# Moving the low part of the output weights from VectorE to GpSimd, behind the last tiles that GpSimd normalises

## The reference, cut to what matters

```python
q = (x @ w_q)              # 32 heads of 128, with rotary embedding
k = (x @ w_k); v = (x @ w_v)   # 8 heads, each serves 4 query heads
lk = ((x @ w_lq) @ w_lk); lv = (x @ w_lv)   # a second, latent set of 32 heads
attn = causal_attn(q, k, v); lat = causal_attn(q, lk, lv)   # softmax over keys
y = attn @ w_o + lat @ w_lo
x = layernorm(x + y)
x = layernorm(x + one_expert_of_eight(x))   # routed, rank 16
```

## Time and profile before

| what | value |
|---|---|
| median of 3 runs | 2124.37 us (2123.72 to 2124.85) |
| time of the profiled execution | 2122.39 us |
| span of its profile | 2120.6 us |
| mean granted TensorE clock | 0.994 of full speed |
| TensorE matmul busy | 2026.5 us, 96% |
| VectorE busy | 1409.2 us, 66% |
| GpSimd busy | 1060.2 us, 50% |
| ScalarE busy | 1044.6 us, 49% |

### The profile page before, as it was taken

One profiled execution on the slowest core, in us unless ns is written; L12 is line 12 of the kernel. 1 busy time (PEld: TensorE's weight loads), 2 busy tenths in 40 slices (PEclk: granted clock), 3 DMA queues, 4 the chain that ended last, 5 costly groups with the idle time before them and its releaser, 6 DMA issues.

```text
span 2120.6 us, 39951 instructions
## 1 busy us (share of the span) xinstructions
PE 2026.5 (96%) x12832; PEld 1824.3 (86%) x12832; DVE 1409.2 (66%) x3404; ACT 1044.6 (49%) x2461; POOL 1060.2 (50%) x873
## 2 busy tenths in 40 slices
PE   6999999999999999999999999999999999999995
PEld 5988889888898888988898898988989888898883
DVE  5757757576675757757577675767757576575766
ACT  3644626355363644626356373554626456273651
POOL 4536465364644537445364554536455364653630
PEclk9999999999999999999999999999999999999998
DMA  5010010100001000010100001010010100100001
GB/s 169 1 33 11 2 54 1 43 1 31 24 1 43 2 32 24 1 43 1 54 1 21 23 1 54 1 33 11 2 54 1 33 11 21 34 1 31 1 11 40
DMA packets 19367, 50.86 MB, mean 24 GB/s; under 512 B 5824, under 2 KB 7872, under 8 KB 19008
## 3 DMA queue, kind: packets, MB, share of 16 engines
q1 hardware_dynamic: 19136, 48.00, 6.8%
HBM read 45.89 MB, written 2.10 MB: 23 GB/s over the span
## 4 chain that ended last, share of the span: by engine, by line
PE 45%; issue 27%; POOL 24%; DVE 3%; POOLq 0%; ACT 0%; DVEq 0%; ACTq 0%
POOL probs L672 14%; PE ps L315 13%; PE ps L316 13%; PE ps L317 13%; PE ps L402 6%; POOL probs L663 4%; POOL ql_lo L667 4%; POOL pt_lo L648 1%; DVE pt_lo L679 1%; DVE stats L804 0%; POOLq L671 0%; PE ps L495 0%; PE ps L510 0%; POOL wlk_lo L654 0%; DVE probs L715 0%
## 5 line engine op out<-in xcount | busy, mean ns | idle before, releaser
L672 POOL TENSOR_TENSOR probs<-probs,inv_sum 128x640 f32<-128x640 f32 (+7 forms) x512 | 586.3, 1147 | 493.8 <-DVE inv_sum L746 493.1
L679 DVE TENSOR_TENSOR pt_lo<-ps,pt_hi 128x512 fp32r<-128x512 f32 (+3 forms) x768 | 401.6, 551 | 202.8 <-ACT pt_hi L517 199.6
L549 ACT ACTIVATE probs<-probs,neg_max 128x640 f32<-128x640 f32 (+7 forms) x512 | 397.6, 777 | 163.5 <-DVE neg_max L739 163.5
L517 ACT ACTIVATE pt_hi<-ps 128x512 fp32r<-128x512 f32 (+3 forms) x768 | 347.1, 486 | 185.3 <-PE ps L402 171.9
L739 DVE CUSTOM_DVE_ANT_0 probs<-ps,mask 128x640 f32<-128x640 f32 (+7 forms) x512 | 384.1, 753 | 57.6 <-PE ps L317 37.2
L315 PE MATMUL ps<-pt_hi,val_hi 128*128 128x256 f32 (+1 forms) x1280 | 371.0, 290 | 31.2 <-DVE pt_lo L679 31.2
L316 PE MATMUL ps<-pt_lo,val_hi 128*128 128x256 f32 (+1 forms) x1280 | 359.7, 281 | 0.0
L317 PE MATMUL ps<-pt_hi,val_lo 128*128 128x256 f32 (+1 forms) x1280 | 358.8, 280 | 0.0
L402 PE MATMUL ps<-ident,probs 128*128 128x128 f32 x2304 | 337.2, 274 | 15.4 <-POOL probs L672 13.3
L402 PEld LDWEIGHTS ps<-ident,probs 128*128 128x128 f32 x2304 | 266.1, 140 | 49.8 <-POOL probs L672 18.7
L315 PEld LDWEIGHTS ps<-pt_hi,val_hi 128*128 128x128 f32 x1280 | 242.5, 189 | 56.5 <-issue 55.0
(11 more groups left out here) (107 smaller groups left out, 4214.7 us busy)
## 6 DMA issues: line engine op xcount, KB each, us to landing
raw<-wo SPq DMA_DIRECT2D x32, 512.0 KB, 3.3
raw<-wq SPq DMA_DIRECT2D x16, 512.0 KB, 3.3
raw<-wlv SPq DMA_DIRECT2D x16, 512.0 KB, 3.9
raw<-wkv SPq DMA_DIRECT2D x8, 512.0 KB, 3.5
acc<-xT SPq DMA_DIRECT2D x4, 512.0 KB, 5.9
acc<-x SPq DMA_DIRECT2D x1, 2048.0 KB, 7.6
wlk_raw<-wlk SPq DMA_DIRECT2D x16, 128.0 KB, 4.0
out<-acc SPq DMA_DIRECT2D x8, 256.0 KB, 2.4
```

What stands on the lines that cost most here:

```text
L517: return nc.scalar.activation(dst, src, ACT.Copy)
L549: nc.scalar.activation(dst, dst, ACT.Exp, bias=neg_max[:, n % 8:n % 8 + 1], scale=-1.0, accum_out=row_sum[:, n % 8:n % 8 + 1]).then_inc(q[ ...
L672: nc.gpsimd.tensor_tensor(b, b, inv_sum[:, k % 8:k % 8 + 1].to_broadcast([P, b.shape[-1]]), ALU.mult).then_inc(q["normed"], 1)
L679: return nc.vector.tensor_tensor(dst, src, h, ALU.subtract)
```

## The change: three subtractions of each pair go from VectorE to GpSimd

A table `LO_AFTER` names tiles 29, 30 and 31. GpSimd, right after it multiplies one of them, waits for `wo_hi` and makes the low part of the weights of part 0, 1 or 2. VectorE no longer does. The start value of the semaphore `wo_lo` is set by GpSimd instead of VectorE. ScalarE's and TensorE's lists are as they were.

```diff
+LO_AFTER = (TILES - 3, TILES - 2, TILES - 1)
...
@@ block.gpsimd
             pool.sem_inc(q["wlk_lo_made"], SEED)
+            pool.sem_inc(q["wo_lo"], SEED)
...
                         nc.gpsimd.tensor_tensor(b, b, inv_sum[:, k % 8:k % 8 + 1].to_broadcast([P, b.shape[-1]]),
                                                 ALU.mult).then_inc(q["normed"], 1)
+                        if k in LO_AFTER:
+                            part = LO_AFTER.index(k)
+                            src, h, l = output_weights(part, pair)
+                            pool.wait_ge(q["wo_hi"], per_pair(g, pair, len(OUT_PARTS), part + 1))
+                            nc.gpsimd.tensor_tensor(l, src, h, ALU.subtract).then_inc(q["wo_lo"], 1)
...
@@ block.vector
-            dve.sem_inc(q["wo_lo"], SEED)
...
                 lo(l, ps[:, O_BANKS[m % len(O_BANKS)], 256 * (m % 2):256 * (m % 2) + 256], h).then_inc(q["o_lo_made"], 1)
-                if m in OUT_AFTER:
-                    part = OUT_AFTER.index(m)
-                    src, h, l = output_weights(part, pair)
-                    dve.wait_ge(q["wo_hi"], per_pair(g, pair, len(OUT_PARTS), part + 1))
-                    lo(l, src, h).then_inc(q["wo_lo"], 1)
```

## The result

| kernel | median | of runs | profiled execution | ratio to before (95%) |
|---|---|---|---|---|
| before | 2124.19 us | 4 (one more than above) | 2122.39 us | |
| changed | 2217.57 us | 4 (2217.29 to 2218.38) | 2217.29 us | 1.044 (1.0425 to 1.0456) |

The changed kernel is 4.4% slower. The forecast was 2213 us, 4.2% slower, with a range of 2191 to 2224 us. Of the runs further down two were far off, one of 10825 us (part 0 alone, 8 runs) and one of 2517 us (part 0 with TensorE's new order, 6 runs), and the medians leave them out.

A forecast was written before the change was run, and what follows sets the result against it. TensorE, busy 96%, was taken to bound the kernel through its waits. Waits of 69.9 us plus clock falls of 18.4 us, 88.3 us on 2122.39 us, gave 2210.7 us; with the median 1.98 us higher, 2213 us, range 2191 to 2224 us.

The forecast's parts named there:

- I take none: VectorE freed of its subtractions: gain at TensorE's wait for tile 30 at most 8.5 us, costed at nothing.
- sentence on cover: At tile 30: its multiplication ends at 132.3, TensorE turns it from 132.38; without GpSimd's cover, any lateness would be TensorE's.
- Part 1: GpSimd's subtraction ahead of tile 31's multiplication waits for ScalarE, so TensorE stands 3.72 us a pair.
- this refilling: Refilling TensorE's pipeline after the wait for tile 31, counted only in the bounds of 3.5 and 3.9 us.
- Part 2: At the pair's end, GpSimd's subtraction finishes later than VectorE's, making TensorE wait 0.65 us longer.
- The clock: Behind the new gap, TensorE's clock falls in 12 of 16 pairs at 1.53 us each, 18.4 us.
- The rule of the Trainium skill: Idle gaps between matmul bursts halve the clock; every pair would see a fall, 94.4 us instead of 88.3 us.
- the interpolation between two gaps: Last-stage falls came 5.1 and 2.0 us after idling began; 3.6 us lies halfway, so half the pairs fall.
- The rival of a low level that lasts twice as long: Low clock reaches into the output tiles, 3.1 us a pair beside the waits: 120 us, 2244 us; chance 0.05.
- The clock did not hold: Rival: behind the new gaps the clock holds or falls in few pairs, only waits count: 2194 us; chance 0.20.
- Nothing was absorbed: Rival: TensorE's later waits for VectorE shrink, by at most 35.9 us: 2177 us; chance 0.05.
- the faster case: Rival: VectorE without part 0 frees TensorE's banks sooner, tile 30's 0.53 us wait goes: 2116 us; faster or cancelled 0.03.

The follow-up runs named there:

- part 0 alone: Against the kernel before, GpSimd makes only the part 0 subtraction and VectorE keeps parts 1 and 2: 2120.39 us, ratio 0.9974.
- part 0 with TensorE's new order: Kernel before with GpSimd making only part 0, and TensorE doing steps 0 and 1 of the first two output tiles, then both last steps: 2109.13 us.
- five repeats: Changed kernel with the third output tile's early step computed five more times in TensorE's gap, 15 more matmuls a pair: 2192.43 us.
- part 2 alone: Against the kernel before, GpSimd makes only part 2, behind tile 31, and VectorE keeps parts 0 and 1: 2131.95 us, ratio 1.0031.
- two repeats: Changed kernel with the third output tile's early step computed two more times in TensorE's gap, 6 more matmuls a pair: 2201.22 us.
- part 1 alone: Against the kernel before, GpSimd makes only part 1, ahead of tile 31, and VectorE keeps parts 0 and 2: 2210.10 us, ratio 1.0395.

## Why the prediction was right

**What bounds.** TensorE's waits, read at the end of a pair, as said. GpSimd's busy share rose by one point and told nothing.

**Part 0.** "I take none" is the step that failed, by 3 us. The bound beside it, 8.5 us, was fair. The prediction put the wait at tile 30 down to ScalarE and to TensorE's own turning, although its own sentence on cover had GpSimd's multiplication ending just before TensorE turned the tile. That multiplication waited for an inverse sum, and this one stood behind part 0 on VectorE. That the subtraction fits into GpSimd's gap held, 1.28 us for 1.30, but it is now what tile 30 waits for.

**Part 1.** 3.72 us a pair was forecast, 3.69 us measured; each link is where it was put: GpSimd 0.08 us behind ScalarE, 2.34 us instead of 2.40, tile 31 in 0.40 us, TensorE 0.13 us behind it instead of 0.06. TensorE lost 0.18 us more than the wait, though. It turned tile 31 and began the next product 0.21 us later, at full clock too (140.32 and 140.52 with five repeats), where before the two were 0.03 us apart (135.42 and 135.45). Before, the load for that product began with the turning, at 135.42; now it begins at 139.81, 0.20 us behind the turning. The prediction had this refilling in its bounds and not in its sum.

**Part 2.** 0.65 us was forecast, and 0.63 us measured with part 2 alone.

**The waits together.** 16 x (3.69 + 0.18 + 0.63) = 72 us, against 69.9. Without a fall of the clock, that is what the 10 such pairs of the kernel with two repeats show: 11.26 - 6.74 = 4.52 us each from the high part of part 1 to the first addition (their tile 31 is 0.02 us later, left in).

**The clock.** It was sized at 12 falls of 1.53 us, 18.4 us. There were 16. In twelve pairs the stretch is 12.6 us in the mean against 11.25 us without a fall, 1.4 us; in the four with the long fall it is 13.8 us, 2.5 us. 12 x 1.4 + 4 x 2.5 = 27 us, and filling the gap gave back 25.1 us. The size of one fall was nearly right (1.53 us, measured 1.4 to 1.5), and their number and the long ones were not: to take 12 of 16 between two gaps that say different things was a guess. The rule of the Trainium skill that stood beside the sum (TensorE: Matmul & The Clock Gate, section Why this matters for your kernels) was nearer than the interpolation between two gaps: at 3.5 us, a fall in every pair. The rival of a low level that lasts twice as long came true in a quarter of the pairs, at 1.1 us more for each and not in all at 3.1.

**The sum.** 72 + 27 - 3 (part 0) - 3 (the open wait) = 93 us; measured are 2217.29 - 2122.39 = 94.9 us between the two profiled executions. The rest lies ahead of the first pair's end (1.1 us) and behind the last (0.7 us), where I followed no row; the end of the first pair alone falls between 134.6 and 137.0 us in the ten profiles. The forecast's 88.3 us had too small a clock and neither of the two gains: two errors that partly cancelled, so it was by luck that the total was nearer than its terms.

**The rivals.** The clock did not hold. Nothing was absorbed: TensorE's waits for VectorE fell from 35.9 to 28.1 us, but 16 of the 80 became waits for GpSimd. The mechanism of the faster case was real and worth 3 us: part 0 alone is 0.26% faster (0.15 to 0.37%), though half of that is the open wait.

## What to carry to other kernels

An engine that is half idle has an order all the same: before work is given to it, find what stands behind the new instruction in its queue, and compare when its operand is ready with when that next instruction is needed. Put a step that waits behind the urgent short one, not ahead of it. The gaps of 3.5 us in TensorE cost 1.4 us or more beyond their length here, so look at the granted clock behind every new gap.

## What the runs showed of the hardware that I had not expected

Whether the clock falls is not told by the length of a gap alone. At 2.15 us, repeated 16 times in one execution, it fell in 6 and held in 10. At 3.5 us it fell in all, and the low level then lasted 3.4 us in twelve pairs and 6.8 us in four, though TensorE was at work in the same way behind each; with part 1 alone it fell in all 16 again, for 6.8 us in two. In the gap of 1.7 us in the middle of every second pair it held in all ten profiles, 80 of 80. Work that is thrown away can pay: 3.45 us of matmuls in a gap of 3.7 us made the kernel 25 us faster.
